# Latent attention by heads in one unrolled pipeline, in place of a looped stage by phases

## The chip, the cores and the metric

The kernel runs on one core of one Trainium2 chip. Its engines are TensorE (PE, with PEld for its weight loads), VectorE (DVE), ScalarE (ACT), GpSimd (POOL) and SyncE (SP), which issues most of the loads. The metric is device time in microseconds from start to end of one execution.

## The reference

Four cross attention layers follow each other over a batch of 2: x is 2 x 512 x 512, the context is 2 x 1024 x 512. Only the attention of the last one (L3, "latent attention") is touched. Its 512 queries per batch come from x, its 1536 keys and values from the context (1024 lines, some blocked by an integer mask) and from x itself (512 lines, never blocked). There are 16 heads of 32:

```python
h = jnp.concatenate([x, latents], axis=1)              # 1024 + 512 lines
q = (latents @ q_w + q_b).reshape(b, k_len, NH, DH)
kv = (h @ kv_w + kv_b).reshape(b, p + k_len, NH, DH, 2)
kmat, v = (kv[..., 0], kv[..., 1])
attn = jnp.einsum('bkhd,bnhd->bhkn', q, kmat) / DH
attn = jnp.where(full_mask[:, None, None, :], attn, -jnp.inf)
attn = jax.nn.softmax(attn.astype(jnp.float32), axis=-1).astype(q.dtype)
attn_out = jnp.einsum('bhkn,bnhd->bkhd', attn, v).reshape(b, k_len, H)
attn_out = attn_out @ out_w + out_b + residual
```

## The kernel before

The program is a list of stages that runs once per batch: load, L0, `grouped` (L1), two `wide` stages (L2) with norms, an MLP, then the latent stage `narrow("l3", ...)`, a norm and the last MLP. Each stage ends in `barrier`. Every engine has its own instruction list in a written order; semaphores tie the lists together. No scheduler moves anything.

To keep fp32 accuracy with fp32r matmuls, a matrix is held as a pair hi and lo, and `mm3` issues three matmuls per product (lines 146 to 148). For a head, the score matmul contracts over 96 rows: 32 of hi, lo and hi again of k against hi, hi and lo of q (`ks`, `qs`). Two more rows hold minus the row's maximum, so that the same contraction with 98 rows gives scores less their maximum.

`narrow` runs a hardware loop of 4 passes (`Fori(0, C)`), each over 4 heads, in the order of the list `plan`:

- Projections (PE lines 146 to 148): k and v of the 4 heads over 1536 keys and q, 84 matmuls of 512 columns. ACT evicts each twice (967, 969; 974, 976) and DVE forms the low halves (1045, 1049).
- Per head, `ks` and `qs` are stacked by selection matmuls on PE (854, 856, 865, 867) and evicted by ACT (990, 994).
- Score part: for each head and each of 4 tiles of 128 queries, three matmuls (886) fill three PSUM banks, and one DVE instruction (1056) adds the mask and takes the maximum over 1536 columns. DVE then writes the negated maxima (1069, 1072) and PE adds them as rows (871).
- Probability part: for each of the 12 tiles of 128 keys and each head, PE computes the transposed scores (904), ACT takes the exponential (1008), DVE adds the tiles into `zt` (1086), PE multiplies by v (916) and sums `zt` with ones (932). At the end DVE takes the reciprocal (1101), scales (1106) and splits (1108); the output product `o` is done in the next pass, added by 1115.

The score part has no exponentials and the probability part has no maxima. At the stage's start POOL builds the selection matrices (754 to 781), and SP waits for them (`sel_done`) before it loads the first weights (733).

## Time and profile before

| | us |
|---|---|
| median of 3 runs (4539.2 to 4545.69) | 4541.96 |
| profiled execution | 4537.67 |
| its span, first to last instruction | 4535.9 |
| PE busy in the span | 4039.0 (89%) |
| DVE busy | 2724.5 (60%) |
| ACT busy | 1959.4 (43%) |
| POOL busy | 1154.2 (25%) |

### The profile page before, as it was taken

To read this page: it belongs to the slowest core of one execution; us is meant where nothing else is said; L and a number is where in the kernel's file an instruction comes from. 1 tells how busy PE (TensorE), PEld (TensorE's weight loads), DVE (VectorE), ACT (ScalarE), POOL (GpSimd) and SP (SyncE) were. 2 spreads that over 40 slices of the span, in tenths; PEclk is the share of its full clock that TensorE was granted. 3 is DMA by queue.
4 is the path that set the end of the run, shared out by engine and by line. 5 is a ranking of instruction groups with operands and counts; after the bars stand their busy time and mean duration, and the time that the engine had idled before them with its cause. 6 is when DMAs were issued, how large, how long until landed. Compare 5 with 4: busy or idle time off the path is not lost.

```text
span 4535.9 us, 58856 instructions
## 1 busy us (share of the span) xinstructions
PE 4039.0 (89%) x21522; PEld 3042.6 (67%) x21522; DVE 2724.5 (60%) x4236; ACT 1959.4 (43%) x3460; POOL 1154.2 (25%) x1228
## 2 busy tenths in 40 slices
PE   6899699997999987898878996999979999879988
PEld 5655488886888865554665554888868888655546
DVE  2588556556565564666525885566565565646665
ACT  2488344433344322555125883344343443225541
POOL 1542213223132133000216422133131232220002
PEclk9999799998999999899889997999989999988989
DMA  1211101101011021000223101011010110210002
GB/s 66 61 37 19 47 26 42 29 30 42 26 42 35 25 68 42 10 2 0 77 74 70 30 17 47 26 42 43 17 47 22 43 42 17 77 33 10 2 0 86
DMA packets 159931, 167.00 MB, mean 37 GB/s; under 512 B 17921, under 2 KB 122566, under 8 KB 159690
## 3 DMA queue, kind: packets, MB, share of 16 engines
q1 hardware_dynamic: 144330, 148.00, 10.7%
...
## 4 chain that ended last, share of the span: by engine, by line
PE 69%; DVE 13%; issue 6%; ACT 6%; POOL 2%; DVEq 1%; DMA 1%; POOLq 0%; SPq 0%; ACTq 0%
PE ps L146 17%; PE ps L148 16%; PE ps L147 16%; PE ps L1755 4%; PE ps L1369 3%; PE ps L904 3%; DVE w_pt_lo L1887 3%; DVE w_mx L1870 3%; PE ps L1381 2%; PE ps L886 2%; PE ps L916 2%; PE ps L1357 1%; DVE l_pt L1056 1%; POOL g_qs L1239 1%; ACT w_p L1814 1%
## 5 line engine op out<-in xcount | busy, mean ns | idle before, releaser
L1887 DVE TENSOR_TENSOR w_pt_lo<-ps,w_pt_hi 128x512 fp32r<-128x512 f32 x512 | 335.0, 686 | 156.4 <-ACT w_pt_hi L1821 156.4
L1676 POOL CAST w_wo_hi<-w_raw 128x1024 fp32r<-128x1024 f32 x32 | 35.1, 1096 | 1321.8 <-PE ps L148 1321.8
L1821 ACT ACTIVATE w_pt_hi<-ps 128x512 fp32r<-128x512 f32 x512 | 281.6, 596 | 200.9 <-PE ps L1755 200.9
L1494 DVE CUSTOM_DVE_ANT_0 g_units<-ps,g_mask 128x1024 f32<-128x1024 f32 x256 | 311.4, 1218 | 81.7 <-PE ps L1357 81.7
L1870 DVE TENSOR_REDUCE w_mx<-ps 128x1 f32<-128x1024 f32 x256 | 312.1, 1219 | 31.4 <-PE ps L148 31.2
L1755 PE MATMUL ps<-ident,w_p 128*128 128x128 f32 x2048 | 279.1, 275 | 39.8 <-DVE w_pt_lo L1887 39.8
L1369 PE MATMUL ps<-ident,g_units 128*128 128x128 f32 x2048 | 291.8, 284 | 20.2 <-ACT g_turned L1448 17.7
L1440 ACT ACTIVATE g_units<-g_units,g_nmx 128x1024 f32<-128x1024 f32 x256 | 294.9, 1152 | 19.7 <-DVE g_nmx L1494 17.0
L1755 PEld LDWEIGHTS ps<-ident,w_p 128*128 128x128 f32 x2048 | 235.2, 140 | 96.6 <-DVE w_pt_lo L1887 67.5
L1369 PEld LDWEIGHTS ps<-ident,g_units 128*128 128x128 f32 x2048 | 221.8, 143 | 100.4 <-issue 63.7
L146 PE MATMUL ps<-w_wv_hi,CT_hi 128*128 128x256 f32 x1024 | 285.0, 278 | 0.0
L148 PE MATMUL ps<-w_wv_hi,CT_lo 128*128 128x256 f32 x1024 | 284.9, 278 | 0.0
L147 PE MATMUL ps<-w_wv_lo,CT_hi 128*128 128x256 f32 x1024 | 284.9, 278 | 0.0
L1814 ACT ACTIVATE w_p<-ps,w_nm 128x1024 f32<-128x1024 f32 x256 | 281.5, 1100 | 0.0
L1812 ACT ACTIVATE w_ex<-w_xl,w_nm 128x1 f32<-128x1 f32 x256 | 75.8, 296 | 417.6 <-DVE w_nm L1876 417.6
L1846 DVE SCALAR_TENSOR_TENSOR w_k_lo<-ps,cols,w_k_hi 128x512 fp32r<-128x512 f32 x128 | 96.1, 751 | 246.7 <-ACT w_k_hi L1796 246.7
L1056 DVE CUSTOM_DVE_ANT_0 l_pt<-ps,l_mask 128x1536 f32<-128x1536 f32 x128 | 218.1, 1755 | 11.7 <-PE ps L886 9.1
L146 PE MATMUL ps<-CT_hi,w_wk_hi 128*128 128x512 f32 x512 | 204.2, 399 | 19.9 <-DVE w_xk_hl L1834 19.9
L146 PE MATMUL ps<-w_pt_hi,w_v_hi 128*128 128x512 f32 x512 | 217.6, 425 | 0.0
L146 PE MATMUL ps<-w_k_hi,w_q_hi 128*128 128x512 f32 x512 | 208.7, 408 | 0.0
L148 PE MATMUL ps<-CT_hi,w_wk_lo 128*128 128x512 f32 x512 | 203.8, 398 | 0.0
L147 PE MATMUL ps<-CT_lo,w_wk_hi 128*128 128x512 f32 x512 | 202.8, 396 | 0.0
...
## 6 DMA issues: line engine op xcount, KB each, us to landing
...
g_qs<-g_q_hi POOLq DMA_DIRECT2D x256, 32.0 KB, 1.8
...
```

What stands on the lines that cost most here:

```text
L146: pe.matmul(o, a[0], b[0], start=start, stop=False, skip_group_check=True)
L147: pe.matmul(o, a[0], b[1], start=False, stop=False, skip_group_check=True)
L148: return pe.matmul(o, a[1], b[0], start=False, stop=stop, skip_group_check=True)
L1056: dve.tensor_tensor_reduce(unused[:, m % s_slots, :].rearrange("p (h w) -> p h w", h=n_hf), ps[:, s0_:s0_ + n_hf, :], madd[:, lt if row_ma ...
L1369: i = pe.transpose(ps[:, T_BANK + h, v * P:(v + 1) * P], units[:, k % U, (4 * h + v) * P:(4 * h + v + 1) * P], ident[:, :])
L1440: act.activation(units[:, k % U, :], units[:, k % U, :], ACT.Exp, bias=nmx[:, k % U:k % U + 1], scale=-1.0, accum_out=z[:, k // 32 % 2, lt ...
L1494: dve.tensor_tensor_reduce(units[:, q % U, :].rearrange("p (h w) -> p h w", h=2), ps[:, 2 * (q % 2):2 * (q % 2) + 2, :], mask[:, q % 4, :] ...
L1755: i = pe.transpose(ps[:, T_BANK + tn % 2, lt * P:(lt + 1) * P], prob[:, u, lt, v * P:(v + 1) * P], ident[:, :])
L1814: act.activation(prob[:, u, lt, :].rearrange("p (h w) -> p h w", h=2), ps[:, S_BANK + 2 * (sn % 2):S_BANK + 2 * (sn % 2) + 2, :], ACT.Exp, ...
L1821: act.activation(pt.h[:, x[2] % 4, :], ps[:, T_BANK + tn % 2, :], ACT.Copy).then_inc(t_hi, 1)
L1870: dve.tensor_reduce(mx[:, u, lt:lt + 1], ps[:, S_BANK + 2 * (sn % 2):S_BANK + 2 * (sn % 2) + 2, :], AX.XY, ALU.max).then_inc(max_own, 1)
L1887: dve.tensor_tensor(pt.l[:, x[2] % 4, :], ps[:, T_BANK + tn % 2, :], as_f32(pt.h[:, x[2] % 4, :]), ALU.subtract).then_inc(t_free, 1)
```

## The change

`narrow` is removed and the latent stage is written anew as `latent()`; the other stages only share some of its semaphores. The 16 heads run in one unrolled sequence of slots: head n has 12 slots j, one for each tile of 128 keys. In slot j all engines work on the probabilities of head n and on the maxima of head n+1.

- Scores: pieces of 128 queries x 512 keys, each in one of banks 0 to 2. PE puts 2, 1, 2, 2, 2, 1, 2 of the next head's 12 pieces in slots 0 to 6. DVE takes each maximum alone (`dve_max`, 1778); the mask is now a row of the contraction (97 rows).
- The negated maxima become two more rows through PE (1643) into a bank of their own (7) and an ACT copy, at slot 10.
- The transposed score tiles alternate between banks 3 and 4; ACT exponentiates them into 13 places of `pt`; the product with v comes in three groups of 4 tiles, after slots 5 and 9 and in slot 1 of the next head.
- Sums over tiles: DVE adds tiles 0 to 5 in three instructions on contiguous places (1796, 1799, 1801) at slot 9; POOL adds the six others and DVE's sum into `zs` (1552, 1561).
- `ks` and `qs` are stacked by DMAs between parts of SBUF that POOL issues (1541, 1542), six per head, in a ring of three; selection matrices and their matmuls are gone.
- v is projected once per batch for all heads, before the first head, straight into the layout that the product needs; k and q of the next 4 heads, and reciprocal (`zq`), `fold` and output products (`o`) of the last 4, are put into slots through bank 6.

```diff
-        def narrow(tag, acc, dh, rep, keys, scale, c_bq, c_bk, c_bv, w_q, w_k, w_v, w_o, bo, row_mask):
...
-                            i.then_inc(score.full, 1)
...
+        def latent():
...
+            vd = sb(own, tag + "_vd", [P, KT, D])
+            ks = sb(own, tag + "_ks", [P, 3, KEYS], F32R)
+            qs = sb(own, tag + "_qs", [P, 3, NQ], F32R)
...
+            pt = sb(own, tag + "_pt", [P, KT + 1, NQ])
...
+            T_BANK_, O_BANK, W_BANK, M_BANK = 3, 5, 6, 7
+            S_IN, PV_AT, TAIL = (2, 1, 2, 2, 2, 1, 2), {5: 0, 9: 1}, 2
+            pieces, n = {}, 0
+            for j, k in enumerate(S_IN):
+                pieces[j], n = range(n, n + k), n + k
...
+            def spread(pool, b, hd):
+                c, u = divmod(hd, U)
+                if hd >= 3:
+                    pool.wait_ge(st_full, (b * HEADS + hd - 2) * KT)
+                elif hd == 2:
+                    pool.wait_ge(s_full, b * HEADS * LT * HF + 1)
+                pool.wait_ge(kq_done, b * KQ + kq_at["q", c] + 1)
+                pool.wait_ge(kq_done, b * KQ + kq_at["k", c, HF - 1] + 1)
+                rows = slice(u * DH, (u + 1) * DH)
+                for blk in range(3):
+                    at_ = slice(DH * blk, DH * blk + DH)
+                    pool.dma_start(ks[at_, hd % 3, :], (kd.h, kd.l, kd.h)[blk][rows, :]).then_inc(head_ready[hd % 2], 16)
+                    pool.dma_start(qs[at_, hd % 3, :], (qd.h, qd.h, qd.l)[blk][rows, c % 2, :]
+                                   ).then_inc(head_ready[hd % 2], 16)
+
...
+            def pool_z(pool, b, hd, part):
+                n, u = b * HEADS + hd, hd % U
+                for i in (range(3), range(3, 6))[part]:
+                    if i == 0:
+                        if hd // U:
+                            ring_wait(pool, b, ("zq", hd // U - 1))
+                        pool.wait_ge(e_done, n * KT + HALF + 2)
+                        pool.tensor_tensor(zs[:, u, :], pt[:, HALF + 1, :], pt[:, HALF + 2, :], ALU.add).then_inc(z_pool, 1)
+                        continue
+                    if i < 5:
+                        pool.wait_ge(e_done, n * KT + HALF + 2 + i)
+                        more = pt[:, HALF + 2 + i, :]
+                    else:
+                        pool.wait_ge(z_dve, n * 3 + 3)
+                        more = pt[:, HALF, :]
+                    pool.wait_ge(z_pool, n * 6 + i)
+                    pool.tensor_tensor(zs[:, u, :], zs[:, u, :], more, ALU.add).then_inc(z_pool, 1)
...
+                spread(pool, b, 0)
+                spread(pool, b, 1)
+                for n in range(HEADS + 1):
+                    if n:
+                        pool_z(pool, b, n - 1, 0)
+                    if n + 2 < HEADS and (n + 2) % U:
+                        spread(pool, b, n + 2)
+                    if n:
+                        pool_z(pool, b, n - 1, 1)
+                    if n == 0:
+                        split_raw(pool, b, ("q", 1))
...
+            def pe_rows(pe, b, hd):
+                if hd == 0:
+                    for i_ in range(2):
+                        pe.wait_ge(v_out[i_], (b + 1) * (KT // 2))
+                pe.wait_ge(max_done, b * HEADS + hd + 1)
+                upto(pe, rows_done, b * HEADS + hd)
+                for lt in range(LT):
+                    i = pe.matmul(ps[:, M_BANK, lt * P:(lt + 1) * P], nmx[:, lt, :], ident_r[:, :],
+                                  start=True, stop=True, skip_group_check=True)
+                i.then_inc(rows_full, 1)
...
+                for n in range(-1, HEADS + TAIL):
+                    for j in range(KT):
+                        for s_ in pieces.get(j, ()) if n + 1 < HEADS else ():
+                            hd, (lt, h) = n + 1, divmod(s_, HF)
+                            if s_ == 0:
+                                pe.wait_ge(head_ready[hd % 2], (b * (HEADS // 2) + hd // 2 + 1) * 6 * 16)
+                            g = (b * HEADS + hd) * LT * HF + s_
+                            upto(pe, s_free, g - 2)
+                            pe.matmul(ps[:, h, :], qs[0:KS, hd % 3, lt * P:(lt + 1) * P],
+                                      ks[0:KS, hd % 3, h * 512:(h + 1) * 512],
+                                      start=True, stop=True, skip_group_check=True).then_inc(s_full, 1)
+                        if j == 1 and 0 <= n - 1 < HEADS:
+                            pe_pv(pe, b, n - 1, 2)
+                        if 0 <= n < HEADS:
+                            g = (b * HEADS + n) * KT + j
+                            if j == 0:
+                                pe.wait_ge(rows_done, b * HEADS + n + 1)
+                            upto(pe, e_done, g - 1)
+                            pe.matmul(ps[:, T_BANK_ + g % 2, :], ks[0:KM, n % 3, j * P:(j + 1) * P], qs[0:KM, n % 3, :],
+                                      start=True, stop=True, skip_group_check=True).then_inc(st_full, 1)
+                            if j in PV_AT:
+                                pe_pv(pe, b, n, PV_AT[j])
+                        for x, ks_of in slices.get((n, j), []):
...
+                            if n:
+                                act.wait_ge(pv_done, (m - 1) * 3 + j // 4 + 1)
+                                if j < HALF:
+                                    act.wait_ge(z_dve, m * 3 - (2 if j < 3 else 0))
+                                else:
+                                    act.wait_ge(z_pool, (m - 1) * 6 + max(j - HALF, 1))
+                            act.activation(pt[:, tile_at(j), :], ps[:, T_BANK_ + (m * KT + j) % 2, :], ACT.Exp,
+                                           bias=zero_col[:, :], scale=SCALE).then_inc(e_done, 1)
+                        if j == 2 and 0 <= n - 1 < HEADS:
+                            hd = n - 1
...
+            def dve_max(dve, b, hd, s_):
+                g, (lt, h) = (b * HEADS + hd) * LT * HF + s_, divmod(s_, HF)
+                dve.wait_ge(s_full, g + 1)
+                dve.tensor_reduce(mxs[:, hd % 2, lt, h:h + 1], ps[:, h, :], AX.X, ALU.max).then_inc(s_free, 1)
+
+            def dve_negate(dve, b, hd):
+                n, s_ = b * HEADS + hd, hd % 2
+                dve.wait_ge(s_free, (n + 1) * LT * HF)
+                upto(dve, rows_full, n)
+                dve.tensor_reduce(mx[:, s_, :], mxs[:, s_, :, :], AX.X, ALU.max).then_inc(max_own, 1)
+                dve.wait_ge(max_own, n * 2 + 1)
+                dve.tensor_scalar(nmx[:, :, 97], mx[:, s_, :], -1.0, None, ALU.mult).then_inc(max_own, 1)
+                dve.wait_ge(max_own, n * 2 + 2)
+                dve.scalar_tensor_tensor(out=nmx[:, :, 98], in0=mx[:, s_, :], scalar=-1.0,
+                                         in1=as_f32(nmx[:, :, 97]), op0=ALU.mult,
+                                         op1=ALU.subtract).then_inc(max_done, 1)
+
+            def dve_z(dve, b, hd):
+                m = b * HEADS + hd
+                dve.wait_ge(e_done, m * KT + HALF)
+                dve.wait_ge(pv_done, m * 3 + 2)
+                dve.tensor_tensor(pt[:, 3:6, :], pt[:, 0:3, :], pt[:, 3:6, :], ALU.add).then_inc(z_dve, 1)
+                dve.wait_ge(z_dve, m * 3 + 1)
+                upto(dve, z_pool, m * 6)
+                dve.tensor_tensor(pt[:, HALF, :], pt[:, 3, :], pt[:, 4, :], ALU.add).then_inc(z_dve, 1)
+                dve.wait_ge(z_dve, m * 3 + 2)
+                dve.tensor_tensor(pt[:, HALF, :], pt[:, HALF, :], pt[:, 5, :], ALU.add).then_inc(z_dve, 1)
...
+                for n in range(-1, HEADS + TAIL):
+                    for j in range(KT):
+                        for s_ in pieces.get(j, ()) if n + 1 < HEADS else ():
+                            dve_max(dve, b, n + 1, s_)
+                        if j == 7 and n + 1 < HEADS:
+                            dve_negate(dve, b, n + 1)
+                        if j == 9 and 0 <= n < HEADS:
+                            dve_z(dve, b, n)
+                        for x in evicts.get((n, j), []):
...
-        narrow("l3", acc3, 32, 1, NK + NQ, 1.0 / 32, at["qb_3"], at["kb_3"], at["vb_3"], t["L3_xattn_q_w"],
-               t["L3_xattn_kv_w"], None, t["L3_xattn_out_w"], t["L3_xattn_out_b"], False)
+        latent()```

The next rows show PE before, in the probability part of `narrow` (its register rows belong to the waits): 904 is a transposed score tile, 916 the product with v.

```order
L904 MATMUL ps<-l_qs,l_ks 128x512
L75 REGISTER_ALU
L904 MATMUL ps<-l_qs,l_ks 128x512
L75 REGISTER_ALU
L904 MATMUL ps<-l_qs,l_ks 128x512
L75 REGISTER_ALU
L904 MATMUL ps<-l_qs,l_ks 128x512
L916 MATMUL ps<-l_pt,l_v 32x512 x4
```

And PE now, slots 0 to 4 of a head: 1682 is a transposed score tile of head n, 1672 a score piece of head n+1, 1654 the product with v of head n-1.

```order
L1672 MATMUL ps<-h_ks,h_qs 128x512 x2
L1682 MATMUL ps<-h_qs,h_ks 128x512
L1672 MATMUL ps<-h_ks,h_qs 128x512
L1654 MATMUL ps<-h_pt,h_vd 32x512 x4
L1682 MATMUL ps<-h_qs,h_ks 128x512
L1672 MATMUL ps<-h_ks,h_qs 128x512 x2
L1682 MATMUL ps<-h_qs,h_ks 128x512
L1672 MATMUL ps<-h_ks,h_qs 128x512 x2
L1682 MATMUL ps<-h_qs,h_ks 128x512
```

Score pieces, which stood in a part of their own, now stand between the tiles.

DVE before, at the same place of the probability part (1086 adds a tile to the sums):

```order
L1086 TENSOR_TENSOR l_zt<-l_pt 128x512 [waits l3_tile_free]
L75 REGISTER_ALU
L1084 ISA [waits l3_tile_free]
L1086 TENSOR_TENSOR l_zt<-l_zt,l_pt 128x512 [waits l3_added]
L75 REGISTER_ALU
L1084 REGISTER_ALU [waits l3_tile_free]
L1086 TENSOR_TENSOR l_zt<-l_zt,l_pt 128x512 [waits l3_added]
```

DVE now, one head's round and the start of the next (1778 maxima, 1784 to 1788 negation, 1754 the low half of a projection, 1796 to 1801 sums of tiles):

```order
L1778 TENSOR_REDUCE h_mxs<-ps 128x1 [waits h_s_full] x12
L1784 TENSOR_REDUCE h_mx<-h_mxs 128x4 [waits h_rows_full,h_s_free]
L1786 TENSOR_SCALAR h_nmx<-h_mx 128x4 [waits h_max_own]
L1788 SCALAR_TENSOR_TENSOR h_nmx<-h_mx,h_nmx 128x4 [waits h_max_own]
L1754 SCALAR_TENSOR_TENSOR h_q_lo<-ps,cols,h_q_hi 128x512 [waits h_kq_hi]
L1796 TENSOR_TENSOR h_pt<-h_pt 128x1536 [waits h_pv_done,h_e_done]
L1799 TENSOR_TENSOR h_pt<-h_pt 128x512 [waits h_z_pool,h_z_dve]
L1801 TENSOR_TENSOR h_pt<-h_pt 128x512 [waits h_z_dve]
L1778 TENSOR_REDUCE h_mxs<-ps 128x1 [waits h_s_full] x12
```

The 12 maxima of the next head stand behind the three sums of this one, and the sums wait for exponentials and for a product with v.

## Rows read from the trace of the kernel before

**Rows 1.** Windows of the latent stage: three stretches, then all of it in either batch.

```profile
core 0: us, PE busy (x) PEld busy (x) DVE busy (x) ACT busy (x) POOL busy (x), PEclk, DMA share, GB/s
1739.80:1763.00 23.20, 2.39 (x17) 1.75 (x17) 6.23 (x11) 2.28 (x4) 17.20 (x43) 0.65 0.28 80
1791.80:1826.00 34.20, 26.86 (x110) 19.48 (x109) 30.66 (x42) 12.51 (x20) 8.03 (x12) 0.89 0.11 32
1826.00:1866.00 40.00, 38.57 (x193) 16.42 (x192) 26.83 (x39) 29.95 (x50) 0.00 (x0) 0.92 0.00 1
1739.80:2163.00 423.20, 352.54 (x1548) 210.33 (x1548) 255.63 (x363) 208.49 (x340) 44.85 (x82) 0.90 0.04 12
3996.60:4424.50 427.90, 355.67 (x1548) 212.75 (x1548) 256.82 (x368) 209.99 (x341) 44.60 (x82) 0.89 0.04 12
```

**Rows 2.** Groups by line, 1739.8 to 2163 us: count, busy us, mean ns, idle before.

```profile
L1056 DVE CUSTOM_DVE_ANT_0 l_pt<-ps,l_mask 128x1536 f32<-128x1536 f32 x64 | 109.1, 1755 | 6.2 <-PE ps L886 5.0
...
L1101 DVE RECIPROCAL l_zt<-ps 128x512 f32<-128x512 f32 x4 | 13.4, 3358 | 4.8 <-PE ps L932 4.8
...
L1069 DVE TENSOR_SCALAR l_nmx<-l_mx 128x4 fp32r<-128x4 f32 x16 | 5.6, 347 | 0.9
```

**Rows 3.** Timeline of DVE, score part: start us, us, engine, line, operation.

```profile
1794.55 1.75 DVE L1056 CUSTOM_DVE_ANT_0 l_pt<-ps,l_mask 128x1536 f32<-128x1536 f32 x1
1796.22 1.75 DVE L1056 CUSTOM_DVE_ANT_0 l_pt<-ps,l_mask 128x1536 f32<-128x1536 f32 x1
```

**Rows 4.** Timeline of DVE and of ACT in the probability part.

```profile
1833.08 4.91 DVE L1086 TENSOR_TENSOR l_zt<-l_zt,l_pt 128x512 f32<-128x512 f32 x8 [1.22 <-ACT l_pt L1008]
...
1832.26 9.37 ACT L1008 ACTIVATE l_pt<-ps,l_mcol 128x512 f32<-128x512 f32 x16 [1.30 <-PE ps L904]
```

**Rows 5.** Timeline of PE in the probability part.

```profile
1833.90 1.34 PE L904 MATMUL ps<-l_qs,l_ks 98*128 98x512 f32 x4
1835.17 1.06 PE L916 MATMUL ps<-l_pt,l_v 128*32 128x512 f32 x8
1836.17 1.39 PE L904 MATMUL ps<-l_qs,l_ks 98*128 98x512 f32 x4
```

**Rows 6.** Timeline of POOL and of PE at the stage's start.

```profile
1739.82 0.53 POOL L754 MEMSET l_selq_hi<- 128x512 f32 x1 [20.87 <-DVEq L232]
1741.69 0.95 POOL L756 MEMSET l_nmx<- 128x1024 f32 x1
...
1762.74 0.61 POOL L800 CAST l_wq_hi<-l_raw_q 128x512 fp32r<-128x512 f32 x1
1763.49 1.28 POOL L804 TENSOR_TENSOR l_wq_lo<-l_raw_q,l_wq_hi 128x512 fp32r<-128x512 f32 x1
...
1762.93 0.79 PE L146 MATMUL ps<-CT_hi,l_wkv_hi 128*128 128x512 f32 x1 [19.82 <-POOL l_wkv_lo L804]
...
1768.75 0.39 PE L147 MATMUL ps<-CT_lo,l_wkv_hi 128*128 128x512 f32 x1
1768.98 0.39 PE L148 MATMUL ps<-CT_hi,l_wkv_lo 128*128 128x512 f32 x1
```

**Rows 7.** Timeline of POOL and DVE in the MLP before; then all of line 2129.

```profile
1684.31 1.45 POOL L2071 TENSOR_TENSOR mlp_w_lo<-mlp_raw,mlp_w_hi 128x512 fp32r<-128x512 f32 x1
1684.64 1.67 DVE L2129 TENSOR_TENSOR mlp_g_lo<-mlp_g,mlp_g_hi 128x512 fp32r<-128x512 f32 x1
...
L2129 DVE TENSOR_TENSOR mlp_g_lo<-mlp_g,mlp_g_hi x64: 691/1668/1671, 1653.7 to 4526.1; 128x512 fp32r<-128x512 f32 x64
```

**Rows 8.** Timeline of POOL and DVE in a wide stage.

```profile
1027.17 2.41 POOL L1681 TENSOR_TENSOR w_wo_lo<-w_raw,w_wo_hi 128x1024 fp32r<-128x1024 f32 x1
...
1028.16 1.23 DVE L1870 TENSOR_REDUCE w_mx<-ps 128x1 f32<-128x1024 f32 x1 [0.76 <-PE ps L148]
```

**Rows 9.** Line 1239: the DMAs that POOL issues in the grouped stage; and their size.

```profile
L1239 POOL DMA_DIRECT2D g_qs<-g_q_hi x256: 487/487/586, 173.4 to 2672.8; - x128
...
g_qs<-g_q_hi POOLq DMA_DIRECT2D x256, 32.0 KB, 1.8
```

887 lines of the change are left out of this document (337 added, 550 removed).

## The prediction

> **What bounds the kernel now.** I read the windows first, because the change touches one stage that runs twice. The latent stage takes 423.2 us in the first batch and 427.9 in the second, 851.1 together [rows 1]. Inside it no engine is full: in the second batch PE is recorded busy for 356 of 428 us, DVE for 257, ACT for 210, POOL for 45. The stretches of one pass say why. In the score part (34.2 us) DVE is busy for 30.7 and ACT for 12.5. In the probability part (40.0 us) ACT has 30.0, DVE 26.8, and PE's record is full. So the stage is a row of phases, each with a bound of its own, and the engine that limits one is idle in the next. Then I read the timelines for pitches, since a duration overlaps its neighbour's. One DVE instruction over 1536 columns comes every 1.67 us (1794.55 to 1796.22) [rows 3]; 512-column ones come at 4.91/8 = 0.61 us and exponentials at 9.37/16 = 0.586 us [rows 4]. PE does four score tiles and one group of products (four of them, recorded as x8) in 1836.17 - 1833.90 = 2.27 us, of which the products are about 1.0 [rows 5]. A full-speed fp32r matmul of 512 columns costs 1768.98 - 1768.75 = 0.23 us [rows 6]. Last, PE idles for 19.8 us at the stage's start, until 1762.93, behind POOL's setup [rows 6].
>
> **The change part by part.** Per batch the new stage is a start, 15 rounds of length T, the last head, and an end. A round is one head's probabilities beside the next head's maxima.
>
> *Start.* POOL's setup becomes memsets of 4608, 1536 and 512 columns. The slope is (0.95 - 0.53)/512 = 0.82 ns a column with 0.1 on top, so 5.8 us; with drains 6.3. Then one cast (0.61) and one subtraction (1.28) [rows 6], 8.4 us in all instead of 23.1. PE then does k and q for the first heads (48 matmuls) and v for 8 of 12 tiles (96): 144 x 0.23 = 33, and about 2 for a slow first ten matmuls, because the granted clock in the first stretch was 0.65 [rows 1]. That is 43. Twelve score pieces and the four other v tiles, 60 x 0.23 = 14, reach 57; the last eviction, the rows of maxima and their copy add 2.5. First probabilities at 59.5 us. The loads and the v split on ACT and DVE lie beside this. DMA stacking of head 0 needs k and q only and lies beside the v tiles.
>
> *A round on DVE*, the engine with the longest list in it:
> (a) 12 maxima at 0.61: 7.4 us. No row has a 512-column maximum; below, 1.67/3 = 0.56 [rows 3] makes it 6.7, and above, the least single record, 0.69 [rows 7], make it 8.3. I take the pitch of rows 4.
> (b) Negation, three small instructions that wait for each other: the longest is 0.35 [rows 2]; 0.8 together, 8.2 so far.
> (c) The sums wait for the second group of products. PE reaches slot 6 when piece 8 has been reduced (5.5) and goes on at the exponentials' 0.586; the products of slot 9 end at about 9.1.
> (d) Sums: a 1536-wide one at the 1.67 of rows 3, two at 0.69: 3.1 with their waits for each other, 12.3.
> (e) Projections' low halves, reciprocal (3.36 [rows 2]), scaling, output additions: 3 x 0.75 + 0.75 + 3.36 + 0.7 + 0.75 + 4 x 0.7 = 10.6 per four heads, 2.6 a head, of which 0.6 fits in the gap before the sums. 14.3.
> (f) The other engine's port. In the MLP a DVE subtraction with two SBUF operands starts 0.33 us after a POOL one of the same kind and takes 1.67 us instead of 0.69; it ends 0.55 after POOL's end, and 1.67 is the median of all 64 [rows 7]. So it waits until POOL's instruction is over. A maximum out of PSUM isn't held: 1.23 us for 1024 columns in the middle of a POOL subtraction [rows 8]. In the new round both engines' sums start near the eighth exponential, POOL's at about 7.6. If POOL gets in before each of DVE's first two, DVE is late by two POOL additions less what they covered already: 2 x 1.28 less 0.2, 2.4 us. Bounds: 0, and 3 x 1.28 = 3.8.
> Sum: T = 16.7 us.
>
> The Trainium skill, SBUF — State Buffer, section "SBUF: two separate sides", calls the shared pair of ports "an exclusive lock, not a bandwidth split", taken for a whole instruction by whoever starts first. By that rule term (f) stands, and it can hit POOL as well as DVE; by proportional sharing it would be nearer to zero, which rows 7 contradict.
>
> *The other engines in a round.* ACT: 12 x 0.586 and two copies of 0.6, and 3.5/4 of evictions: 9.1. PE: 12 pieces and 12 tiles at 0.23, three groups of products at 1.0, rows of maxima 0.8, and per four heads 48 x 0.23 of projections, 2.8 of output products and 2 of reductions, 4.0 a head: 13.3. POOL: 6 additions of 1.28, 6 DMA issues of 0.49 [rows 9], splits of 1.9 in three of four rounds: 12.0, and 3.1 when DVE's sums hold it. All are below 16.7, PE and POOL by little. The removed selection matmuls and double evictions were on the old path and are in the 851.1.
>
> *Last head:* 12 exponentials without maxima, 7.0 and 2 of latency: 9. *End:* POOL's six additions for it lag by 8.2 (10.8 with DVE's sums in between, less 2.6 of exponentials), the sum matmuls 1.0, reciprocal 3.5, scaling, two halves and one fold 3.0, output 3.2: 18.9.
>
> Stage: 59.5 + 9 + 18.9 + 15 T = 87.4 + 15 T = 337.9 us. Twice 675.8, against 851.1: 175 us gained. The profiled execution goes from 4537.67 to 4362; it lies 4.3 below the median, so the forecast on the medians is 4541.96 - 175 = **4367 us**. Every microsecond in T is 30 in the result.
>
> **The rivals.**
> *No collision (T = 14.3).* Both engines' sums may interleave without loss: a DVE reciprocal before them (one head in four) lets POOL finish, and POOL's DMA issues separate its two halves. For it: POOL has only 12 us to do. Against it: rows 7, 64 of 64 in one place. Stage 301.9, gain 247, time 4295.
> *The written order binds (T = 19).* PE has one list: a piece stands behind the tile that waits for ACT, and behind products (1.0) or half a projection (6 x 0.23 = 1.4) that cover more than one maximum of 0.61; three banks hold 1.8 us of work for DVE. With 24 projection matmuls in one head of four, 5.5 us, mostly added, plus some 1.0 in each round from products, T grows by 2.3. For it: PE's list is 13.3 us long. Against it: DVE must be idle, not just late. Stage 372.4, gain 106, time 4436.
> *Slower than before.* The stacking DMAs are 192 KB for k and 64 KB for q, where the row that I have shows 32 KB at 0.49 us [rows 9]. If POOL's issue time grows with the bytes, the six cost 3 x 2.9 + 3 x 1.0 = 11.7 us, POOL's round is 7.7 + 11.7 + 1.4 + 3.1 = 24 us, and exponentials of the next head wait for its additions. Stage 87.4 + 360 = 447, time 4542 + 44 = 4586. It decides from T = (425.5 - 87.4)/15 = 22.5 us. Against it: twice the partitions is all that grows if a row is one piece, 1.0 us each at most, which gives POOL 15 and stays hidden.
> The Trainium skill, DMA: Bandwidth & Descriptors, section "Anatomy of one DMA — SWDGE (gpsimd) path", calls descriptor generation "small, variable". No row here shows a large one; by this rule the slower rival falls.
> *The change doesn't overlap as written* would look like T = 7.4 + 9.1 + 3.1, 19.6, and is inside the second rival.
>
> **How the numbers follow.** Forecast 0.45 (T from 15.3 to 17.7: 4325 to 4397), no collision 0.25, written order 0.22, slower 0.05, anything else 0.03. The range 4285 to 4440 holds the first three but for their far ends: T from 14 to 19.1. A change under 0.2% (9 us) can't be told from none; it needs T near 22.5, 0.02. Faster 0.93, slower 0.05.
>
> **What would show it.** In the new trace the first PE matmul of the stage comes 8 to 9 us after the first memset; 1778 comes at a pitch near 0.61 us; 1796 and 1799 take about 1.3 us more than their least when a line 1561 of POOL runs; POOL's 1541 takes 0.5 to 1.0 us; a round, from one 1796 to the next, is 16 to 17.5 us, longer where k is projected; ACT waits for PE, and PE for DVE's maxima in slots 2 to 6. I am wrong if DVE idles for more than 3 us in a round (then PE's order binds), if 1796 never exceeds 1.8 us (no collision), or if POOL's DMA rows grow past 2 us.

## The result, and the profile after

The changed kernel takes 4508.11 us (median of 4 runs, 4505.49 to 4514.29), the kernel before 4541.13 beside it (4 runs): ratio 0.9932, 95% interval 0.9921 to 0.9944. It is faster by 33 us, not by the 175 forecast; 4508 lies outside the range. The profiled execution took 4514.29 us, with a span of 4512.5.

The windows, columns as in [rows 1], over the stage's start, a stretch of full rounds of the first batch, and the stage in either batch:

```profile
1739.80:1763.00 23.20, 16.59 (x67) 13.15 (x68) 8.64 (x11) 7.38 (x12) 11.45 (x13) 0.85 0.52 170
1816.00:2080.00 264.00, 215.09 (x865) 112.23 (x865) 200.73 (x259) 124.42 (x194) 163.83 (x169) 0.86 0.21 46
1739.80:2151.40 411.60, 328.94 (x1296) 182.00 (x1296) 269.88 (x354) 168.45 (x262) 221.46 (x225) 0.83 0.20 47
3989.10:4402.70 413.60, 329.15 (x1296) 182.16 (x1296) 270.75 (x359) 169.75 (x262) 221.89 (x225) 0.83 0.20 47
```

The stage takes 411.6 and 413.6 us where 337.9 was forecast. Line 1796, the first of DVE's three sums, starts at 1815.90 for head 0, at 2101.82 for head 14 and at 2123.99 for head 15. So the 14 rounds between heads 0 and 14 took 285.9, 20.42 us each (forecast 16.7), and the last 22.17. Per batch the miss is 14 x 3.72 = 52.1 in the rounds, 5.5 in the last, 7.5 before the first sums (76.1 against 68.6) and 8.6 behind the last (27.4 against 18.8): 73.7.

The maxima and sums of DVE and the adds of POOL, least/median/longest in ns (they answer to the pitches of [rows 3, 4] and the collision of [rows 7]):

```profile
L1778 DVE TENSOR_REDUCE h_mxs<-ps x384: 671/680/695, 1788.2 to 4346.9; 128x1 f32<-128x512 f32 x192
L1796 DVE TENSOR_TENSOR h_pt<-h_pt x32: 1757/2572/2850, 1815.9 to 4373.4; 128x1536 f32<-128x1536 f32 x32
L1799 DVE TENSOR_TENSOR h_pt<-h_pt x32: 691/1650/1661, 1817.8 to 4375.2; 128x512 f32<-128x512 f32 x32
L1801 DVE TENSOR_TENSOR h_pt<-h_pt x32: 691/1634/1649, 1819.5 to 4376.8; 128x512 f32<-128x512 f32 x32
L1561 POOL TENSOR_TENSOR h_zs<-h_zs,h_pt x160: 1261/1288/2767, 1814.9 to 4379.7; 128x512 f32<-128x512 f32 x160
```

The waits in that stretch of full rounds, of DVE first, then of PE (us in total, times, longest); line 1672 is a score piece, 1654 a group of products, 1682 a transposed tile:

```profile
DVE h_mxs L1778 <- PE ps L1672: 39.2, 23, 3.4
DVE h_pt L1796 <- PE ps L1654: 11.5, 9, 2.0
DVE h_k_lo L1754 <- ACT h_k_hi L1703: 5.1, 6, 0.8
```

```profile
PE ps L1672 <- DVE h_mxs L1778: 26.7, 10, 3.3
PE ps L1672 <- DMA h_qs<-h_q_lo: 6.0, 3, 2.5
PE ps L1682 <- ACT h_pt L1730: 4.9, 9, 0.6
```

Per round of 20.42 (12.93 of them in 264 us) DVE is busy for 15.5 and idle for 4.9, of which 3.0 go to PE's pieces and 0.9 to the products. And PE waits for DVE as well. The timeline of PE and DVE shows how both can be (start, us):

```profile
1868.09 0.63 PE L146 MATMUL ps<-XT_hi,h_wq_hi 128*128 128x512 f32 x1
...
1868.51 0.63 PE L147 MATMUL ps<-XT_lo,h_wq_hi 128*128 128x512 f32 x1
1868.94 0.63 PE L148 MATMUL ps<-XT_hi,h_wq_lo 128*128 128x512 f32 x1
...
1876.83 2.74 DVE L1796 TENSOR_TENSOR h_pt<-h_pt 128x1536 f32<-128x1536 f32 x1 [0.32 <-PE ps L1654]
...
1878.86 0.40 PE L1672 MATMUL ps<-h_ks,h_qs 97*128 97x512 f32 x1
...
1879.60 1.65 DVE L1799 TENSOR_TENSOR h_pt<-h_pt 128x512 f32<-128x512 f32 x1
...
1881.90 2.48 DVE L1778 TENSOR_REDUCE h_mxs<-ps 128x1 f32<-128x512 f32 x4
1882.63 1.19 PE L1672 MATMUL ps<-h_ks,h_qs 97*128 97x512 f32 x2 [1.90 <-DVE h_mxs L1778]
```

During the sums PE fills three banks, then stands for 1.90 us until DVE takes the first maximum. Right behind that the granted clock is at the lower of its two levels:

```profile
1883.50:1890.30 6.80, 6.80 (x26) 2.99 (x25) 4.58 (x8) 3.24 (x5) 4.87 (x6) 0.50 0.27 55
```

What that does to fp32r matmuls, the first three lines of the timeline show. They are from the round before this one, 8.3 us behind a wait of PE of 2.53 us (for the stacked q, until 1859.78), and are 0.42 and 0.43 us apart, where it was 0.23 in [rows 6]. Over the whole stretch the granted clock is 0.86.

### The profile page after: what moved, and what is told of

Read it like the earlier page. It is cut to its first block, busy times and chain, and to the rows that moved or that the text cites. A ratio compares the mean times of both kernels' runs of the same rounds, so it can differ in the third digit from the quotient of the medians.

```text
span 4512.5 us, 55800 instructions
## 1 busy us (share of the span) xinstructions
PE 3995.1 (89%) x21018; PEld 2988.1 (66%) x21018; DVE 2751.4 (61%) x4218; ACT 1878.4 (42%) x3302; POOL 1509.8 (33%) x1514
## 4 chain that ended last, share of the span: by engine, by line
PE 68%; DVE 16%; ACT 5%; issue 5%; POOL 2%; DVEq 1%; DMA 1%; POOLq 1%; SPq 0%; ACTq 0%
PE ps L146 17%; PE ps L148 16%; PE ps L147 16%; PE ps L1167 4%; PE ps L781 3%; DVE w_pt_lo L1299 3%; DVE w_mx L1282 3%; PE ps L1672 2%; PE ps L793 2%; DVE h_pt L1796 2%; PE ps L1682 1%; PE ps L1654 1%; DVE h_mxs L1778 1%; PE ps L769 1%; POOL g_qs L651 1%
## 5 line engine op out<-in xcount | busy, mean ns | idle before, releaser
L1730 ACT ACTIVATE h_pt<-ps,zero_col 128x512 f32<-128x512 f32 x384 | 256.6, 687 | 296.5 <-PE ps L1682 289.7
L1778 DVE TENSOR_REDUCE h_mxs<-ps 128x1 f32<-128x512 f32 x384 | 241.2, 681 | 100.7 <-PE ps L1672 100.4
L146 PE MATMUL ps<-w_wv_hi,CT_hi 128*128 128x256 f32 x1024 | 285.2, 279 | 0.0
L148 PE MATMUL ps<-w_wv_hi,CT_lo 128*128 128x256 f32 x1024 | 285.2, 279 | 0.0
L147 PE MATMUL ps<-w_wv_lo,CT_hi 128*128 128x256 f32 x1024 | 285.1, 278 | 0.0
L1561 POOL TENSOR_TENSOR h_zs<-h_zs,h_pt 128x512 f32<-128x512 f32 x160 | 244.7, 1529 | 35.1 <-ACT h_pt L1730 13.5
L1672 PE MATMUL ps<-h_ks,h_qs 97*128 97x512 f32 x384 | 172.8, 514 | 75.0 <-DVE h_mxs L1778 60.4
L146 PE MATMUL ps<-CT_hi,w_wk_hi 128*128 128x512 f32 x512 | 204.9, 400 | 20.8 <-DVE w_xk_hl L1246 20.8
L146 PE MATMUL ps<-w_pt_hi,w_v_hi 128*128 128x512 f32 x512 | 217.6, 425 | 0.0
```

The source lines that it names most:

```text
L146: pe.matmul(o, a[0], b[0], start=start, stop=False, skip_group_check=True)
L147: pe.matmul(o, a[0], b[1], start=False, stop=False, skip_group_check=True)
L148: return pe.matmul(o, a[1], b[0], start=False, stop=stop, skip_group_check=True)
L1778: dve.tensor_reduce(mxs[:, hd % 2, lt, h:h + 1], ps[:, h, :], AX.X, ALU.max).then_inc(s_free, 1)
```

## The experiments

Times are medians; "gain" is against the changed kernel's 4508.1. The round is the mean from head 0's line 1796 to head 14's, first batch. Intervals are of the ratio to the kernel before, measured beside each run. The gain leaves out how the chips differ: by the ratios e2's would be 14 us in place of 18, and e18 has one run of the kernel before beside it, 4532.1, 9 us under the one beside the changed kernel. A run that moves lines of the kernel has other line numbers than the changed kernel; the text says what each is.

| run | us | ratio (interval) | gain | round |
|---|---|---|---|---|
| changed kernel | 4508.1 | 0.9932 (0.9921 to 0.9944) | | 20.42 |
| e1_pool_after | 4473.0 | 0.9862 (0.9846 to 0.9878) | 35 | 18.85 |
| e2_fill8 | 4490.6 | 0.9902 (0.9886 to 0.9919) | 18 | 19.36 |
| e3_pool_cut (one run) | 4398.8 | | 109 | 17.16 |
| e4_dve_cut (one run) | 4419.3 | | 89 | 17.55 |
| e5_slots | 4534.2 | 0.9987 (0.9978 to 0.9997) | -26 | 20.92 |
| e6_pool_three | 4453.6 | 0.9806 (0.9790 to 0.9822) | 55 | 18.40 |
| e7_both | 4493.2 | 0.9896 (0.9876 to 0.9917) | 15 | 19.71 |
| e8_no_proj (one run) | 4462.9 | | 45 | 18.84 |
| e9_between | 4505.0 | 0.9926 (0.9909 to 0.9943) | 3 | 20.08 |
| e10_slots_klo | 4505.4 | 0.9923 (0.9906 to 0.9939) | 3 | 20.19 |
| e12_zq_later | 4456.9 | 0.9822 (0.9805 to 0.9838) | 51 | 18.11 |
| e13_all | 4503.3 | 0.9920 (0.9904 to 0.9937) | 5 | 20.20 |
| e14_zq_last | 4467.3 | 0.9836 (0.9819 to 0.9853) | 41 | 18.68 |
| e15_zq_last_slots | 4487.4 | 0.9881 (0.9864 to 0.9897) | 21 | 19.45 |
| e16_zq_last_no_proj (one run) | 4440.2 | | 68 | 17.59 |
| e17_zq_last_fill | 4471.2 | 0.9849 (0.9833 to 0.9866) | 37 | 18.64 |
| e18_pool_cut_no_proj (one run) | 4359.0 | | 149 | 15.51 |
| e19_three_out_first | 4447.0 | 0.9799 (0.9783 to 0.9815) | 61 | 18.53 |

### The lock, the clock, and each engine's adds

e1_pool_after, in `pool_z` before the first add:

```diff
+                        pool.wait_ge(z_dve, n * 3 + 3)
```

> POOL begins its sums of a head only when DVE's three are done. Time of the changed kernel is 4508. If the port collision is what DVE's round is longer by (sums take 5.2 us of a round instead of 3.1), T falls by 2.1 to 2.7 us and the time by 63 to 80: about 4435; records of 1796, 1799 and 1801 return to 1.76, 0.69, 0.69. If PE's written order and its fallen clock set the round and the collision only fills time in which DVE would wait anyway, T falls by under 1 us: 4480 or more. A rival: POOL, now later, holds the exponentials of slots 8 to 11 of the next head, and nothing is gained.

e2_fill8, in PE's list at slot 2: eight dummy matmuls of 512 columns (cut).

```diff
+                            for _ in range(8):
+                                pe.matmul(ps[:, M_BANK, :], ident_r[:, :], XT.h[:, 0, :], start=True, stop=True,
...
```

> Eight more matmuls of 512 columns in slot 2 of every round into the idle bank 7, where PE waits for DVE's sums (1.9 to 2.8 us idle there). They compute nothing. If the fall of the granted clock after that wait (pitch 0.43 us instead of 0.23 for the next 4 to 8 us) costs part of each round, T falls by 0.5 to 1.5 us, 4465 to 4493, and the granted clock of the rounds rises from 0.86 to over 0.95. If DVE and the lock alone set the round, the time stays within 10 us of 4508 or rises by what of 8 x 0.23 = 1.8 us isn't inside the wait (up to 50 us).

e3_pool_cut and e4_dve_cut each leave out most of one engine's sums:

```diff
-                    pool.tensor_tensor(zs[:, u, :], zs[:, u, :], more, ALU.add).then_inc(z_pool, 1)
+                    pool.tensor_tensor(zs[:, u, 0:8], zs[:, u, 0:8], more[:, 0:8], ALU.add).then_inc(z_pool, 1)
```

> Five of POOL's six additions per head work on 8 columns instead of 512, so the sums over tiles are left out in part. The collision nearly goes and POOL has 6 us less per round. If the collision is the cause: as with POOL starting after DVE, about 4435. If POOL's own length also held rounds, lower still, under 4415. If neither, 4480 or more.

```diff
-                dve.tensor_tensor(pt[:, 3:6, :], pt[:, 0:3, :], pt[:, 3:6, :], ALU.add).then_inc(z_dve, 1)
+                dve.tensor_tensor(pt[:, 3:6, 0:8], pt[:, 0:3, 0:8], pt[:, 3:6, 0:8], ALU.add).then_inc(z_dve, 1)
...
```

(The third sum is cut to 8 columns likewise.)

> Two of DVE's three sums of tiles work on 8 columns a tile, so these sums are left out in part; what is left is one of 512 columns and two short ones, about 1.0 us and up to 1.3 with one collision instead of 5.2. If DVE's list sets the round, T falls by about 4 us: 4390. If PE's order at half clock sets most of it, T falls by about 2: 4450. If nothing on DVE matters: 4500.

Of e1, DVE's three sums, then PE's wait before the matmul of four heads' sums (`zq`):

```profile
L1797 DVE TENSOR_TENSOR h_pt<-h_pt x32: 1694/1758/2295, 1816.3 to 4327.0; 128x1536 f32<-128x1536 f32 x32
L1800 DVE TENSOR_TENSOR h_pt<-h_pt x32: 691/692/1661, 1818.1 to 4328.8; 128x512 f32<-128x512 f32 x32
L1802 DVE TENSOR_TENSOR h_pt<-h_pt x32: 691/691/1653, 1818.8 to 4329.5; 128x512 f32<-128x512 f32 x32
```

```profile
PE ps L1623 <- POOL h_zs L1562: 15.1, 3, 5.4
```

The three sums, from the first's start to the last's end, fall from 5.23 us a round to 3.27. The collision is shown, and its size is 2.0 us in DVE's list, 2.4 forecast. The round fell by 1.6, between the two theories of that run (2.1 to 2.7, and under 1), and 4473.0 lies between their times. Its rival is part of the reason: POOL is now late once in four heads.

e4 takes 2.6 us out of DVE's list (the sums take 2.65 in place of 5.23) and the round falls by 2.9: DVE's sums are on the path with their whole length. 4419.3 lies between the 4390 and the 4450 of its theories. With POOL's adds all but gone (e3) the round falls by 3.3 us, where DVE's sums are shorter by 1.8; 4398.8 is under the 4415 that was to show that POOL's own length holds rounds too. So e3 prices lock and load of POOL together, not the lock alone. Windows of the same stretch for e3, then e2:

```profile
1816.00:2080.00 264.00, 223.80 (x998) 108.79 (x997) 195.75 (x292) 145.16 (x227) 103.83 (x188) 0.95 0.21 46
```

```profile
1816.00:2080.00 264.00, 230.87 (x1022) 123.94 (x1022) 211.40 (x273) 131.31 (x205) 174.09 (x175) 0.95 0.21 46
```

In e2 the lock stays (the sums take 5.17), the granted clock goes from 0.86 to 0.95, the round falls by 1.1, and 14 to 18 us are won with more work than before, as expected. In e3 the clock is at 0.95 with no dummy at all.

### POOL in time

e6_pool_three waits for DVE only at the first three heads of four; e12_zq_later waits at all heads and puts the matmul of four heads' sums at slot 7; e14_zq_last waits at all heads too and puts it at slot 9, behind DVE's sums.

```diff
+                        if u < 3:
+                            pool.wait_ge(z_dve, n * 3 + 3)
```

> Edit: GpSimd's first add of a head waits for the last of VectorE's three sums, but only at the first three heads of each four; at the fourth GpSimd starts as in the changed kernel, so that the matmul of all four sums is not late. Main theory: it keeps what the wait at all heads gives (sums 3.2 us in place of 5.2, 35 us off) but for one round in four, and gives back most of the 2 us by which rounds after heads 3, 7 and 11 were longer (22.4 us, PE waiting for GpSimd's last add 15.1 us in three rounds): 3 x 2 x 2.5 = 15 us less one lock of 2 x 4 x 2: 4465 us, 4455 to 4474. Rival (the long rounds come from the slices alone, not from GpSimd's lateness): the lock at every fourth head comes back and nothing is won for it, 4480 to 4490 us.

```diff
-                    put(("zq", c - 1), [((n0, 5), ())], (n0, 8))
+                    put(("zq", c - 1), [((n0, 7), ())], (n0, 8))
```

> Edit: GpSimd's first add waits for VectorE's last sum at every head, and PE's matmul of the four sums, for which PE waited 15.1 us in three rounds when GpSimd was late, stands at slot 7 of the head in place of slot 5. Theory: the lock is gone in all rounds and GpSimd's lateness costs PE nothing: against the kernel with the wait at all heads (4473 us) three rounds a batch of 22.4 fall to 19.5: less 18 us, 4455 us, 4440 to 4462. Rival (those long rounds come from exponentials that wait for GpSimd's adds to free their tiles, not from that matmul): 4470 to 4476 us.

```diff
-                    put(("zq", c - 1), [((n0, 5), ())], (n0, 8))
-                    put(("fold", c - 1), [((n0, 10), ())], (n0, 11))
+                    put(("zq", c - 1), [((n0, 9), ())], (n0, 9))
+                    put(("fold", c - 1), [((n0, 11), ())], (n0 + 1, 0))
```

> Edit: GpSimd's wait at all heads, and the matmul of the four sums at slot 9 with its reciprocal behind VectorE's sums of that head; the fold at slot 11 with its eviction in the next head. Theory: with that matmul at slot 7 VectorE still stood 7.6 to 8.8 us between negation and sums in the rounds after heads 3, 7 and 11, where other rounds have 1.6 to 3.9, because the reciprocal ahead of the sums waited for it. Behind the sums it holds nothing up: three rounds a batch of 19.2 to 19.9 us become 16 to 17, the mean round falls from 18.1 to 17.5: 4457 less 2 x 3 x 3 = 4440 us, 4430 to 4448. Rival (GpSimd's late adds hold up the exponentials of the later tiles as well): 4450 to 4460 us.

e12 came as expected, 4456.9 (4440 to 4462 forecast); e6, 4453.6, is 1.4 us better than its range (4455 to 4474), and its rival (4480 to 4490) is out. DVE's three sums in e12, all but free of the lock:

```profile
L1797 DVE TENSOR_TENSOR h_pt<-h_pt x32: 1694/1759/2265, 1814.1 to 4307.1; 128x1536 f32<-128x1536 f32 x32
L1800 DVE TENSOR_TENSOR h_pt<-h_pt x32: 691/692/695, 1815.9 to 4308.9; 128x512 f32<-128x512 f32 x32
L1802 DVE TENSOR_TENSOR h_pt<-h_pt x32: 691/692/1647, 1816.6 to 4309.6; 128x512 f32<-128x512 f32 x32
```

The sums take 3.31 in place of 5.23, and the round falls by 2.3 with every add still done. This is the best price of the lock alone: 1.9 us of it in DVE's list.

e14 missed. The rounds after heads 3, 7 and 11 fell from 19.8, 19.2 and 19.9 in e12 to 13.1, 13.7 and 13.7 us, more than asked; the ones behind them grew from 20.4, 19.6 and 15.2 to 29.5, 27.3 and 22.9. Most of that is the reciprocal and what hangs on it, which changed rounds; each pair is 1.5 to 2.3 us longer in sum. POOL's first add of the next head comes only behind that matmul, PE's fold waits for the reciprocal, and the wait is handed on:

```profile
1887.15 1.72 PE L1623 MATMUL ps<-h_zs,ones 128*32 128x512 f32 x8 [3.16 <-POOL h_zs L1562]
1888.91 3.36 DVE L1762 RECIPROCAL h_rzb<-ps 128x512 f32<-128x512 f32 x1
1890.49 1.27 POOL L1553 TENSOR_TENSOR h_zs<-h_pt 128x512 f32<-128x512 f32 x1
1891.90 2.67 POOL L1562 TENSOR_TENSOR h_zs<-h_zs,h_pt 128x512 f32<-128x512 f32 x2
...
1892.32 1.94 PE L1628 MATMUL ps<-h_parts,h_fold 128*32 128x512 f32 x8 [1.45 <-DVE h_rzb L1762]
```

e17_zq_last_fill puts up to six dummy matmuls (slots 1 and 2, where no slice stands) into e14:

> Edit: the kernel with the matmul of the four sums at slot 9, with three dummy matmuls of 512 columns at slots 1 and 2 where no slice stands. Theory (part of the clock's loss came from the wait behind the locked sums, and is gone with them; the granted clock is 0.93 without fillers): the fillers give at most 5 us, 4433 to 4442. Rival (the half clock after PE's wait is a cost of its own, worth the 17 us that eight dummy matmuls gave before): 4418 to 4428 us.

4471.2 against 4467.3, intervals of the ratio overlapping: no gain, as its theory had it. With the lock away there is less half clock left to win (granted 0.92 without the dummies, 0.94 with them). So the gains of e2 and e1 may be partly the same microseconds; no run has both edits on the changed kernel.

### PE's projection slices

e8_no_proj, in `pe_ring`; e18 has the same beside e3's edit, e16 beside e14's:

```diff
+                if x[0] in "kq" and x[1]:
+                    if ks_of[0] == 0:
+                        i = pe.matmul(ring(x), (wk if x[0] == "k" else wq).h[:, 0, :], XT.h[:, 0, :], start=True, stop=True,
...
```

> Leaves out the key and query projections of the heads behind the first ones: one matmul in place of the twelve of each piece, with all waits, evictions and DMAs kept. Main theory (slices lie on the path): the rounds of 22 to 23 us fall to 18 or 19, those of 19 to 20 by 1 us; a mean round of 20.4 falls to about 18, less 2 x 15 x 2.4 = 72 us: 4436 us, 4410 to 4465. Rival A (lock alone): PE's work is hidden, 4500 to 4510 us. Rival C (PE with less work gets a lower granted clock and gives the gain back): 4490 to 4510 us with a granted clock under 0.8 in the stage.

> Leaves out the key and query projections of the later heads, as before, in the kernel with the matmul of the four sums at slot 9. Alone that took the mean round from 20.4 to 18.8 us. Theory (the lock and PE's list are two costs on one path, VectorE's sums and then its maxima behind PE's pieces): additive, the mean round goes to about 16, less 45 us again: 4395 us, 4385 to 4410. Rival (both gains are one slack): 4425 to 4440 us.

> Leaves out both: five of GpSimd's six adds of a head work on 8 columns, and the later heads' key and query projections are one matmul in place of twelve. Alone the first took the mean round from 20.4 to 17.2 us, the second to 18.8. Theory (PE's list and GpSimd's adds are two costs of the same path, both taken at nothing or too small in the forecast): additive, 17.2 - 1.6 = 15.6 us or less, near the 14.3 forecast for VectorE's list alone: 4399 less 45 = 4354 us, 4340 to 4370. Rival (the projections cost only where GpSimd's lock has made PE wait first): the round stays above 16.8, 4385 to 4400 us.

The four corners of the mean round: 20.42 with both, 18.84 without projections, 17.16 without POOL's adds, 15.51 without either. The effects, 1.58 and 3.26, add up to 4.84 of the 4.91 found, and e18's 4359.0 is in the range of its theory (4340 to 4370). e8's 4462.9 is just inside its range (4410 to 4465), with 1.6 us a round where 2.4 were expected. e8's window has a lower granted clock than the changed kernel's 0.86, and is faster all the same:

```profile
1816.00:2080.00 264.00, 207.92 (x811) 100.00 (x808) 215.15 (x284) 133.81 (x208) 177.36 (x177) 0.81 0.20 46
```

e16 gave 27 us over e14 where 45 were expected, and ends at its rival's 4440: additive it is not there. With POOL late, part of the projections' time would be a wait for POOL anyway; that was not traced.

### Moving work into PE's wait, and DVE's order

e5_slots does the third key piece of the next four heads (k2) and the query piece q at slots 0 and 1, where PE waits, and moves two output pieces from slot 2 to 4. e10_slots_klo has the same for k2 and q(c+2), with DVE's low half of the piece before it ahead of the sums. e7_both is e5 with e6, e15 is e10 with e14.

```diff
-                    put(("k", c + 1, 2), [((n0 + 2, 3), (0, 1)), ((n0 + 2, 4), (2, 3))], (n0 + 2, 5))
+                    put(("k", c + 1, 2), [((n0 + 2, 0), (0, 1)), ((n0 + 2, 1), (2, 3))], (n0 + 2, 2))
```

> Edit: PE's list alone is written otherwise. The second half of the key projection k(c+1) and the query projections q(1) and q(c+2) are read at slots 0 and 1 of a head, where PE now waits for DVE's sums, instead of slots 3 to 7, where they stand before score pieces; two output pieces go from slot 2 to 4. Main theory (the round's length is set by the path from PE's pieces to DVE's maxima, on which PE's slices lie and on which PE runs at half clock after its wait): in the three rounds of four that carry such a slice the time from the end of DVE's sums to the negation (12.2 us in the changed kernel) falls by 1.5 to 2.5 us, the granted clock of the stage rises from 0.86 to 0.9 or more, so 3 x 4 x 2 x 1.2 = about 30 us off: 4478 us, 4465 to 4492. Rival A (the lock between VectorE's sums and GpSimd's adds alone sets the round): the lock is untouched, 4505 to 4511 us. Rival B (PE's work in the first slots only delays the probabilities by what it takes): slower, 4515 to 4530 us.

> Edit: both edits together, the slices at slots 0 and 1 and GpSimd's wait at three heads of four. Main theory: the two act on different parts of the round (the maxima's part and the sums' part), so their gains add up to within a quarter: 4508 less 30 less 43 = about 4435 us, 4415 to 4455. Rival (both only shorten the same wait of PE, so the second gives nothing once the first is made): the better of the two alone, 4465 to 4480 us.

> Edit: k(c+1) second half and q(c+2) at slots 0 and 1 as in the slots kernel, but q(1) stays where it was, and VectorE takes the low part of the piece before it ahead of its sums, so that the one bank of the ring is free when PE comes to slot 0. Theory on the slots kernel's loss (PE waited 4.4 us for that low part, behind the sums, three times a batch, and q(1) at slot 0 put off the first probabilities by 7.6 us): both are gone, what is left is the gain in the rounds after them: 4508 less 2 x (3 x 2) to 2 x (3 x 5) = 4495 us, 4478 to 4500. Rival (projection in front of the pieces delays the maxima by its own 2.4 us or more wherever the bank is free): 4510 to 4525 us.

> Edit: the kernel with the matmul of the four sums at slot 9, and k(c+1) second half and q(c+2) at slots 0 and 1 with the low part ahead of VectorE's sums. Theory: as in the slots run with the low part first, two rounds a batch (heads 5 and 9) fall by 3.4 us, since the DMAs that stack head 4(c+1) go out earlier, and two (heads 4 and 8) rise by 0.8: 4440 less 2 x 5 = 4430 us, 4420 to 4440. Rival (with the lock gone DVE comes to the pieces 2 us earlier and the projection in front of them costs its 2.4 us): 4445 to 4460 us.

All four missed. In e5 the first sums came 7.6 us later (1823.55 against 1815.90), and PE met a wait that I hadn't looked for:

```profile
PE ps L146 <- DVE h_k_lo L1754: 13.3, 3, 4.4
```

The slices share one bank. At slot 0 the bank still holds the piece before, whose low half stands behind DVE's locked sums. e10 takes that away and two rounds fall by 3.4 us each (those from heads 5 and 9, 22.46 and 22.43 to 19.01), but others grow and the 3 us left are within the interval. In e10 PE's wait for the stacked q (6.0 us, three times) is gone as well, with no shorter rounds: the three that had it (from heads 2, 6 and 10) take 56.8 us together, where it was 55.8. Query slices fill its place there, so what the stacking DMAs cost isn't settled; by the wait it is 0.5 us a round at most. e7 and e15 lose 40 and 20 us against e6 and e14: with shorter sums PE has less wait to fill (its wait for maxima is 9.3 us in e6 and 6.2 in e14, against 26.7).

e9_between puts maxima between DVE's sums, two behind the first and one behind the second:

```diff
+                for s_ in (0, 1) if more else ():
+                    dve_max(dve, b, hd + 2, s_)
                 dve.wait_ge(z_dve, m * 3 + 1)
...
```

> Edit: VectorE's order alone. Its three tile sums no longer stand together: the maxima of the next head's score pieces 0 and 1 stand between the first and the second sum, that of piece 2 between the second and the third. No instruction is added or left out. Main theory (the 5 us in which VectorE adds in one go let PE run out of free score banks, PE waits 2 to 4 us, then runs 4 to 8 us at half clock and the maxima wait for it): PE's wait for DVE at the start of the rounds (29.6 us of the matmuls, 53.2 of the weight loads in 286 us) falls to under half, the granted clock of the stage rises from 0.86 to over 0.92, rounds fall by 1.5 to 2: less 2 x 15 x 1.5 = 45 us, 4463 us, 4450 to 4480. Rival A (VectorE's busy time and its lock with GpSimd set the round, PE's clock only fills idle time): 4503 to 4511 us. Rival D (the exponentials wait longer for the sums, which now end 2 us later, and the later products more than give the gain back): 4515 to 4530 us.

```profile
DVE h_mxs L1778 <- PE ps L1672: 45.9, 29, 3.8
```

```profile
PE ps L1682 <- ACT h_pt L1730: 14.9, 12, 4.0
PE ps L1672 <- DVE h_mxs L1778: 12.5, 11, 2.3
```

PE's wait for maxima halved, 26.7 to 12.5, as expected. Its wait for exponentials rose from 4.9 to 14.9, and DVE's for pieces from 39.2 to 45.9. The granted clock didn't rise (0.84), the time is the same within the interval: the main theory of that run fell. 4505.0 is in the range of its rival A, but the waits are those of its rival D, exponentials that wait longer because the sums end later. Here removing one wait of PE didn't shorten the round; its other wait took it. e13_all, the same with e12 and with the low half first, was forecast at 4405 to 4445 and missed by far more: from the first sum's start to the last's end, with three maxima between, it took 6.0 us a round, so POOL started later still, and 46 us of e12's gain went.

> Edit: the last edit (GpSimd's wait at all heads, the matmul of the four sums at slot 7), the maxima of pieces 0 to 2 between the sums, and the low part of a key piece ahead of the sums. Main theory: lock and PE's wait are two costs; rounds of 5.2 + 12.2 + 3.0 = 20.4 become 3.2 + 11 + 3 = 17.5: 4508 less 2 x 15 x 2.9 = 4420 us, 4405 to 4445. Rival (both gains come from the same wait of PE, so that one of them alone gives it all): 4450 to 4465 us.

e19_three_out_first moves one eviction in e6 (head 14, slot 9) ahead of the sums. In the changed kernel PE had stood there with all its list:

```profile
2107.57 0.80 PE L146 MATMUL ps<-h_wo_hi,h_att_hi 128*128 128x512 f32 x1 [5.46 <-DVE acc L1773]
```

> Edit: GpSimd's wait at three heads of four, as before, and at head 14 VectorE adds an output piece ahead of its three sums in place of behind them. Theory (a piece of the one-bank ring that is evicted behind the sums stops PE's whole list: in the changed kernel PE waited 5.46 us there, at 2107.57, and the first tile of the last head came 7 us late): the last full round, 22.2 us in the changed kernel, falls to 17 and the stage by 5 us in either batch: 4454 less 10 = 4444 us, 4438 to 4450. Rival (something else, as GpSimd's sums, ends that round just as late): 4450 to 4458 us.

The last round fell from 19.69 us in e6 to 11.62, so the bank was its cause. Not all of these 8 us reached the end of the stage: from its first memset to its last output piece it is shorter by 2.7 us in the first batch and by 5.7 in the second. POOL began the last head's adds at 2091.42, behind the cast of the output weights, where in e6 it began at 2091.25, behind the exponentials; the matmul of the sums waited for it in both. POOL's rows, e19 and then e6:

```profile
2089.94 1.51 POOL L1528 TENSOR_TENSOR h_wo_lo<-h_raw,h_wo_hi 128x512 fp32r<-128x512 f32 x1 [0.16 <-issue]
2091.42 1.70 POOL L1554 TENSOR_TENSOR h_zs<-h_pt 128x512 f32<-128x512 f32 x1
2093.27 6.88 POOL L1563 TENSOR_TENSOR h_zs<-h_zs,h_pt 128x512 f32<-128x512 f32 x5
```

```profile
2091.25 1.27 POOL L1554 TENSOR_TENSOR h_zs<-h_pt 128x512 f32<-128x512 f32 x1 [3.27 <-ACT h_pt L1732]
2092.67 8.92 POOL L1563 TENSOR_TENSOR h_zs<-h_zs,h_pt 128x512 f32<-128x512 f32 x5
```

4447.0 is in the range of the theory (4438 to 4450), but can't be told from e6's 4453.6 by the intervals. It has the lowest median of all complete versions: 2% under the kernel before, 1.4% under the changed one.

## Why the prediction was wrong

- *The step that failed: that an engine with a shorter list costs nothing.* The forecast counted DVE's list and the lock, and took PE's list at nothing, because it was 13.3 us and T was 16.7. Of the 3.72 us by which a round was longer, the experiments name 1.6 as PE's projection slices (e8; 1.65 between e3 and e18). Another 0.9 are POOL's adds beyond the 2.4 of term (f) (3.3 in e3). The last 1.2 are what is left with neither, 15.51 in e18 against the 14.3 of the forecast without collision. In e18's 14 rounds DVE is busy for 13.3 of 15.5 us and idle for 2.3, of which 0.9 are waits for score pieces and 0.5 for groups of products; the shares weren't parted further.
- *Where in the round.* From the end of the sums the negation begins after 12.2 us, where terms (a) and (e) give 7.4 and 2.0; from there to the next sums it is 3.0, where (b) and (c) give 1.7. DVE's own work was sized right: 15.5 us busy against 7.4 + 0.8 + 3.1 + 2.6 + 2.4 = 16.3. Missing were 4.9 us of idle time, where the sum leaves 0.4. A maximum took 0.68 us, and four in a row 2.48, a pitch of 0.60 as forecast.
- *Term (f), the lock.* Its size in DVE's list was nearly right (2.0 for 2.4 in e1, 1.9 in e12), but it holds the third sum too (1634 for 691 ns), where two were forecast. What it does beyond DVE was missed. POOL is held too (2767 ns for 1288), PE runs out of banks, waits, and goes on at half clock. Its price is 2.3 us a round by e12; e3's 3.3 (109 us in the result) has POOL's load in it too.
- *The second rival, PE's order*, was the nearest in mechanism, but it was not an alternative to the collision, as I had it. Both hold, and they add (e3, e8, e18). Of its 2.3 us, 1.4 were projections, which measured 1.6; the other 1.0, products in each round, is not confirmed as such: DVE's waits for groups of products are 0.9 us a round in the changed kernel.

```profile
DVE h_pt L1803 <- PE ps L1661: 24.1, 9, 14.0
DVE h_pt L1803 <- PE ps L1661: 7.7, 7, 1.8
```

(e18, DVE's waits for groups of products: in 1816 to 2080 us, and in its 14 rounds, 1814 to 2031 us. The wait of 14.0 is in the last round, where DVE has no maxima left to do.)

- *The start.* First PE matmul 8.6 us after the first memset (8.4 forecast), where [rows 6] had 23.1. The first exponential was 6.4 us late; a load of ACT's table, 1.28 us, is one part, the rest wasn't traced. (The recorded terms of the start, 6.3 + 0.61 + 1.28, give 8.2 and not 8.4; it changes nothing.)
- *The end*, 8.6 us over. The output pieces come at a pitch of 2.43 us (2143.21, 2145.64), where I put 0.8: each waits for the one bank, and the clock of 2101.8 to 2151 us is 0.54. That is 4 x 1.6 = 6.5 of the 8.6. The last round's 5.5 us over 16.7 have a cause of this kind as well, an output piece in that bank behind the sums: freed, it gave 8 us in e6's last round (e19).
- *The slower rival* is false. Line 1541 with 192 KB takes what [rows 9] showed for 32 KB:

```profile
L1541 POOL DMA_DIRECT2D h_ks<-h_k_hi x64: 492/509/564, 1764.3 to 4317.5; - x64
```

- One sign given for "I am wrong" came true: DVE idle for more than 3 us in a round. It was 4.9.

The Trainium skill, SBUF — State Buffer, section "SBUF: two separate sides", has the shared ports as a lock for a whole instruction. This case agrees in both directions: DVE's 512-column add takes 691 or 1650 ns with nothing between 0.7 and 1.6 us in lines 1799 and 1801, and POOL's goes from 1261 to 2767.

*Open.* How much of the clock's loss alone is on the path once the lock is gone (e17 says nothing above its error, some 10 us); the last 1.2 us a round, left in e18; the stacking DMAs' 0.5 us a round; and the 5 us at the start. That e3's gain goes beyond e6's by 54 us bounds what POOL's load costs; whether it is its lateness or its remaining locks was not parted.
